# Eight-head gated attention ring: ScalarE's last masked copies, the values' high halves, VectorE's maxima and GpSimd's expert sums in another order

## The chip, the cores and the metric

The kernel runs on one core of one Trainium2 chip. The metric is device time in microseconds (us) of one execution. Six engines' rows appear in the profile: PE and PEld (TensorE's matmuls and weight loads), DVE (VectorE), ACT (ScalarE), POOL (GpSimd) and SP (SyncE). The engines run their own instruction streams in order and wait for each other through semaphores.

## The reference

Four layers run one after the other on `x` (4 batches, 256 tokens, width 128): a gated mLSTM-like attention with 4 heads, a mixture-of-experts attention with 8 heads, a cross attention with 16 heads, and a mixture of 8 feed-forward experts. The change touches the second one only:

```python
def _L0_ffn_ref(x, Wq, Wkv, Ws, Wd, Wo):       # b = 4, t = 256, H, E, DH, K = 8, 5, 64, 3
    ss = sigmoid(x @ Ws).reshape(b, t, H, E);  sd = sigmoid(x @ Wd).reshape(b, t, H, E)
    ms, md = topk_mask(ss, K), topk_mask(sd, K)
    q = einsum('bthed,bthe->bhtd', (x @ Wq)..., sd * md)
    k, v = the same of x @ Wkv with ss * ms
    attn = softmax(einsum('bhid,bhjd->bhij', q * scale, k))
    out = einsum('bhij,bhjd->bihd', attn, v)
    o5 = einsum('bthd,dm->bthm', out, Wo).reshape(b, t, H, E, DIM)
    return einsum('bthem,bthe->btm', o5, md)
```

The last two lines are computed the other way round: first z[t, e, d] = sum over heads h of md[t, h, e] * out[t, h, d], then z is multiplied by `Wo`. Products are kept near float32 by splitting operands into a high and a low float16 half.

## The kernel before, in words

**Tiling.** A batch is two tiles of 128 tokens (i = 0, 1). The 8-head layer goes through the batches in a ring of 12 steps each (`STEPS`), written as a hardware loop of three turns (`Fori(0, B - 1)`) on each engine. One turn has two halves. In the heavy half (steps 5 to 11 of batch b) the engines finish batch b's heads and project the gated queries, keys and values of batch b + 1 (the 30 chunks of `CHUNKS`). In the light half (steps 0 to 4 of batch b + 1, `HEAD_STEPS`) no chunk is projected; the experts' sum z of batch b is made and multiplied by `Wo`, beside the first heads of batch b + 1. The change is in the light half alone.

**What a step does.** In step h TensorE makes the scores of head h + 1 (L536 to L538), multiplies weights and values of head h - 3 (L560 to L562) and transposes the weights of head h - 1 (through the helper on L2056). VectorE takes the negated row maxima of head h (`nm`, L832) and the low half of the transposed weights of head h - 2 (`PTl`, L839). ScalarE copies the high half of the weights of head h - 2 (L691) and takes the exponentials of head h (L696). TensorE's scores of head h + 1 need the exponentials of head h - 1, since two PSUM banks hold the scores in turn. Its transpose of head h - 1 needs the low half of head h - 3, and the first product with the values (head 0, in step 3) needs both low halves of the values and the low half of head 0's weights.

**What else lies in the light half.**
- VectorE makes the copies of the output `ho` masked by experts 0 to 2, three instructions for a tile (`copies_z`, L870), with tile 0 ahead of step 0 and tile 1 behind step 0. Both operands lie in SBUF. Behind step 1 it takes the low halves of the values (`split_v`, two instructions, L826), again with both operands in SBUF.
- ScalarE makes the copies of experts 3 and 4 (`masked`, L711), two heads at a time. The last eight of them, and the high halves of the values (`high_v`, two instructions, L684), stand behind the exponentials of head 0.
- GpSimd sums the copies over heads for both tiles (`attend`, L964 to L967): t is the part of VectorE's copies, u that of ScalarE's. For each tile it waits for both, and then goes in turn over t and u, with a wait for its own writes behind each pair.
- TensorE transposes z of tile 0 behind step 3 and of tile 1 behind step 4, each followed by the product with `Wo` (L596). The rows of x that VectorE adds it to (L876) are what the next half waits for: TensorE takes up scores again only when both tiles are added.

**What sets the order.** Each engine's order is written by hand in `act_b`, `dve_b`, `pool_b` and `pe_b`. `POOL_STEPS_B` counts GpSimd's waits for its own writes in one turn of the loop.

Of the kernel before, what the change touches and what calls it, by code (L numbers as in the profile page):

```python
# [5 lines left out]
ALU = mybir.AluOpType  # L6
# [10 lines left out]
I = S // P  # L17
# [13 lines left out]
H1, E1, DH1, TOP = 8, 5, 64, 3  # L31
# [78 lines left out]
N_W1 = 9  # L110
N_WALL = 17
N_EARLY = 4
DVE_STEPS_B, POOL_STEPS_B, DVE_STEPS_C = 4, 16, 8


def build(nc, x, ctx_in, mask, g_x, g_f, w_i, b_i, w_f, b_f, ln_w, Wq0, Wkv0, Ws, Wd, Wo0,
          gm, bm, gl, bl, Wq1, Wk1, Wv1, Wo1, gate_w, w1, b1, w2, b2, out):
    with ExitStack() as stack:
        m, s, d = Names(), Names(), Names()
# [348 lines left out]
        T1, O1, X1 = 4 + H1, H1 // 2, len(PARTS) * I * E1  # L468
# [201 lines left out]
        def act_b(act):  # L670
# [9 lines left out]
            def high_v(b):  # L680
                act.wait_ge(s.O_ready, b * H1 + RING)
                for i in range(I):
                    act.wait_ge(s.acc_ready, b * SUMS + (4 + i + 1))
                    act.activation(m.v1h[:, i, :, 0:DH1], heads8(m.acc[:, 2, i, :]), ACT.Copy).then_inc(s.v1hi_ready, 1)  # L684
# [18 lines left out]
            def masked(b, o):  # L703

                act.wait_ge(s.O_free, b * O1 + (o + 1 + RING))
                for i in range(I):
                    for e in range(E1 - ACT_E, E1):
                        for h in (2 * o, 2 * o + 1):
                            r = slice(DH1 * h, DH1 * h + DH1)
                            at = G1 + h * E1 + e  # L710
                            ins = act.activation(m.zm[:, i, e - (E1 - ACT_E), r], m.ho[:, i, r], ACT.Copy, scale=m.topm[:, b * I + i, at:at + 1])  # L711
                    if o == O1 - 1:
                        ins.then_inc(s.z_masked, 1)
# [12 lines left out]
            with act.Fori(0, B - 1) as b:  # L726
                for h in range(HEAD_STEPS, STEPS):
                    step(b, h, True)
                    if h > HEAD_STEPS and h % 2 == 0:
                        masked(b, h // 2 - 3)  # L730
                for h in range(HEAD_STEPS):
                    step(b + 1, h, False)
                    if h == 0:
                        high_v(b + 1)
                    if h == 0:
                        masked(b, O1 - 1)
                    if h == 3:
                        copy_z(b, 0)
                    if h == 4:
                        copy_z(b, 1)  # L740
            act.wait_ge(s.z_sum, (B - 1) * I)
            act.wait_ge(s.const, 3)
            for h in range(HEAD_STEPS, STEPS):
                step(B - 1, h, False)
                for head in range(2 * (h - HEAD_STEPS), min(2 * (h - HEAD_STEPS) + 2, H1)):
                    for e in range(E1):
                        n = head * E1 + e
# [43 lines left out]
        def dve_b(dve, ch, stats, between):  # L791
# [33 lines left out]
                    dve.wait_ge(s.v1hi_ready, b * I + (i + 1))  # L825
                    dve.tensor_tensor(m.v1l[:, i, :, 0:DH1], heads8(m.acc[:, 2, i, :]), m.v1h[:, i, :, 0:DH1], ALU.subtract).then_inc(s.v1lo_ready, 1)  # L826

            def step(b, h, more):
                chunks3 = chunks_of(h) if more else ((), (), ())
                if h < H1:  # L830
                    dve.wait_ge(s.S_ready, b * H1 + (h + 1))
# [1 line left out]
                        .then_inc(s.nm_ready, 1)  # L833
                for c in chunks3[0]:
                    gate_products(b + 1, c, SUMS + b * GROUPS + c // E1)
                if 2 <= h < H1 + 2:
                    g = h - 2
                    dve.wait_ge(s.T_hi, b * T1 + (4 + g + 1))
                    dve.tensor_tensor(m.PTl[:, g % 2, :, :].rearrange("p n c -> p (n c)"), bank_T[g % 2][:, :],  # L839
                                      m.PTh[:, g % 2, :, :].rearrange("p n c -> p (n c)"), ALU.subtract).then_inc(s.T_free, 1)  # L840
# [49 lines left out]
            with dve.Fori(0, B - 1) as b:  # L890
                ch.loop(b, DVE_STEPS_B)
                for h in range(HEAD_STEPS, STEPS):
                    step(b, h, True)
                z_group = SUMS + b * GROUPS + SUMS
                copies_z(b, 0, z_group)
                for h in range(HEAD_STEPS):
                    step(b + 1, h, False)
                    if h == 0:
                        copies_z(b, 1, z_group + 1)
                    if h == 1:  # L900
                        split_v(b + 1)
                    if h == 4:
                        add_x2(b, 0)
                add_x2(b, 1)
# [25 lines left out]
        def pool_b(pool, ch, rstd, split):  # L930
# [23 lines left out]
            def attend(b):  # L954
                for k in range(SUMS):
                    sums(b + 1, k)
                for i in range(I):
                    pool.wait_ge(s.z_ready, b * I + (i + 1))
                    pool.wait_ge(s.z_masked, b * I + (i + 1))
                    E0 = E1 - ACT_E  # L960
                    t, u = (a.rearrange("p e (h c) -> p e h c", h=H1) for a in (m.prod[:, i, 0:E0, :], m.zm[:, i, :, :]))
                    z = m.z[:, i, :].rearrange("p (e c) -> p e c", e=E1)
                    for n in (4, 2):
                        pool.tensor_tensor(t[:, :, 0:n, :], t[:, :, 0:n, :], t[:, :, n:2 * n, :], ALU.add)  # L964
                        ch.link(pool.tensor_tensor(u[:, :, 0:n, :], u[:, :, 0:n, :], u[:, :, n:2 * n, :], ALU.add))
                    pool.tensor_tensor(z[:, 0:E0, :], t[:, :, 0, :], t[:, :, 1, :], ALU.add)
                    pool.tensor_tensor(z[:, E0:E1, :], u[:, :, 0, :], u[:, :, 1, :], ALU.add).then_inc(s.z_sum, 1)  # L967
                    pool.wait_ge(s.z_sum, b * I + (i + 1))
                    pool.sem_inc(s.prod_free, 1)

# [1430 lines left out]
```

## Time and profile before

| | us |
|---|---|
| median of 3 runs | 712.01 (707.45 to 712.67) |
| profiled execution | 711.09, its span 709.3 |
| PE busy in the span | 580.5 (82%) |
| DVE busy | 507.1 (71%) |
| POOL busy | 376.5 (53%) |
| ACT busy | 346.4 (49%) |
| granted TensorE clock, mean | 0.893 of full |

Times of the trace are counted from the start of the span. The three light halves start at about 198, 258 and 318 us and are over at about 219, 280 and 338 us. A row of the timeline can stand for several like instructions (xN); the times of such a row reach from the first start to the last end. What stands in brackets is how long the engine had been idle, and which instruction released it.

### The profile page before, as it was taken

The page shows a single profiled execution, that of the slowest core. Times are in us where ns is not written, and L with a number is a line of the kernel's source. Part 1 is how long each engine was busy: PE and PEld are TensorE (multiplying, and loading weights), DVE is VectorE, ACT ScalarE, POOL GpSimd, SP SyncE. Part 2 cuts the span into 40 slices and gives each one's busy share as a digit, 9 for nine tenths or more (in the row PEclk, how much of TensorE's full clock was granted, in tenths as well). Part 3 has the DMA queues.
Part 4 walks back from the last instruction along what each step waited for, and adds up shares of the span by engine and source line. Part 5 has one row for each costly group of instructions (what it writes and reads, how often), then busy time and mean ns, then how long its engine had stood idle before and what let it go on. Part 6 is the DMA issues. An engine that isn't in the chain of part 4 may idle for free. (4 is left out here: it accounts for less than half of the span.)

```text
span 709.3 us, 15705 instructions
## 1 busy us (share of the span) xinstructions
PE 580.5 (82%) x5739; PEld 391.0 (55%) x5739; DVE 507.1 (71%) x1069; ACT 346.4 (49%) x750; POOL 376.5 (53%) x340
## 2 busy tenths in 40 slices
PE   5399865769868859976747879999999999888897
PEld 5277622245344425434643446777677677666795
DVE  4936899967974982995885677776776767577653
ACT  2333300044243243425722668877877887625554
POOL 5514345663763755667447556666866665732221
PEclk9999997858968985996656999999999999999998
DMA  6311000020000000000220000000000000000000
GB/s 186 109 43 30 31 30 0 0 90 1 2 0 1 0 0 0 0 0 0 61 61 30 2 1 2 2 1 3 2 2 2 2 2 2 2 1 1 2 14 22
DMA packets 14175, 13.12 MB, mean 18 GB/s; under 512 B 3120, under 2 KB 11936, under 8 KB 14112
## 3 DMA queue, kind: packets, MB, share of 16 engines
q1 hardware_dynamic: 14112, 12.25, 5.9%
q8 instruction: 43, 0.70, 0.4%
q14 instruction: 20, 0.16, 0.1%
HBM read 11.72 MB, written 0.52 MB: 17 GB/s over the span
## 5 line engine op out<-in xcount | busy, mean ns | idle before, releaser
L1468 POOL TENSOR_TENSOR attn<-work,attn 128x512 f16<-128x512 f32 (+1 forms) x96 | 141.9, 1480 | 85.7 <-ACT attn L1275 85.7
L807 DVE TENSOR_TENSOR work<-banks,gatev 128x512 f32<-128x512 f32 x120 | 79.0, 682 | 17.0 <-PE banks L513 16.5
L1368 DVE TENSOR_REDUCE nmax<-banks 128x2 bf16<-128x1024 f32 x64 | 77.8, 1216 | 2.8 <-PE banks L1120 1.7
L511 PE MATMUL banks<-weights,xbTh 128*128 128x512 f16 x120 | 50.2, 418 | 28.4 <-DVE work L807 26.3
L1272 ACT ACTIVATE work<-banks,maskbias 128x512 f32<-128x512 f32 x64 | 44.2, 691 | 41.1 <-PE banks L1146 41.1
L2056 PE MATMUL banks<-ident,work 128*128 128x128 f32 x276 | 51.8, 325 | 8.6 <-DVE work L2256 3.0
L942 POOL TENSOR_TENSOR work<-work 128x512 f32<-128x512 f32 x24 | 30.4, 1268 | 43.9 <-DVE work L807 41.7
L1164 PE MATMUL banks<-work,attn 128*128 128x65 f16 x512 | 51.9, 196 | 1.6 <-POOL attn L1468 1.0
L1164 PEld LDWEIGHTS banks<-work,attn 128*128 128x128 f16 x512 | 48.3, 100 | 8.0 <-POOL attn L1468 4.5
L1165 PE MATMUL banks<-work,attn 128*128 128x65 f16 x512 | 52.0, 196 | 0.0
L1166 PE MATMUL banks<-work,attn 128*128 128x65 f16 x512 | 51.9, 196 | 0.0
L512 PE MATMUL banks<-weights,xbTh 128*128 128x512 f16 x120 | 49.9, 416 | 0.0
L513 PE MATMUL banks<-weights,xbTl 128*128 128x512 f16 x120 | 49.5, 412 | 0.0
L1165 PEld LDWEIGHTS banks<-work,attn 128*128 128x128 f16 x512 | 48.0, 99 | 1.8
L1166 PEld LDWEIGHTS banks<-work,attn 128*128 128x128 f16 x512 | 48.1, 99 | 0.0
L2056 PEld LDWEIGHTS banks<-ident,work 128*128 128x128 f32 x276 | 38.6, 168 | 16.8 <-issue 4.9
L511 PEld LDWEIGHTS banks<-weights,xbTh 128*128 (+1 forms) x120 | 12.1, 101 | 63.8 <-DVE work L807 56.7
L1275 ACT ACTIVATE attn<-banks,maskbias 128x512 f16<-128x512 f32 x64 | 44.2, 691 | 0.0
L946 POOL TENSOR_TENSOR work<-work 128x512 f32<-128x512 f32 x24 | 30.4, 1266 | 23.5 <-DVE work L810 23.4
L696 ACT ACTIVATE work<-banks,nm 128x256 f32<-128x256 f32 x64 | 26.5, 470 | 31.5 <-DVE nm L832 31.5
L536 PE MATMUL banks<-attn 64*128 64x256 f16 x64 | 22.2, 362 | 23.8 <-ACT work L696 14.7
L2023 POOL TENSOR_TENSOR weights<-stage,weights 128x1024 f16<-128x1024 f32 (+1 forms) x14 | 32.8, 2343 | 14.2 <-ACT weights L1917 13.6
(328 smaller groups left out, 1874.7 us busy)
## 6 DMA issues: line engine op xcount, KB each, us to landing
stage<-in_L_ffn_w SPq DMA_DIRECT2D x8, 512.0 KB, 4.0
stage<-in_L_ffn_Wkv SPq DMA_DIRECT2D x4, 640.0 KB, 4.1
stage<-in_L_ffn_Wq SPq DMA_DIRECT2D x2, 640.0 KB, 4.6
xt<-in_x SPq DMA_DIRECT2D x1, 512.0 KB, 4.4
ct<-in_ctx SPq DMA_DIRECT2D x1, 512.0 KB, 5.6
wo<-in_L_xattn_Wo SPq DMA_DIRECT2D x1, 512.0 KB
stage<-in_L_xattn_Wv SPq DMA_DIRECT2D x1, 512.0 KB, 3.6
stage<-in_L_xattn_Wq SPq DMA_DIRECT2D x1, 512.0 KB, 3.5
```

Source lines behind the costliest of these rows:

```text
L511: pe.matmul(o, xh, wh, start=True, stop=False)
L512: pe.matmul(o, xh, wl, start=False, stop=False)
L513: pe.matmul(o, xl, wh, start=False, stop=True).then_inc(s.pj_ready, 1)
L807: dve.tensor_tensor(heads8(m.prod[:, k, e, :]), heads8(bank_pj[c % 2][:, :]), wide(g, DH1), ALU.mult).then_inc(s.prod_ready, 1)
L1164: pe.matmul(o, ph, vh, start=(kt == 0), stop=False)
L1165: pe.matmul(o, ph, vl, start=False, stop=False)
L1166: ins = pe.matmul(o, pl, vh, start=False, stop=(kt == KT - 1))
L1272: act.activation(full, src, ACT.Exp, scale=DH2 ** -0.5, bias=bias)
L1275: act.activation(hi, src, ACT.Exp, scale=DH2 ** -0.5, bias=bias).then_inc(s.c_exp_done, 1)
L1368: dve.tensor_reduce(m.nmax[:, p % 2, i, :], banks[:, 6:8, :], AX.X, ALU.max, negate=True).then_inc(s.c_max_done, 1)
L1468: pool.tensor_tensor(m.Pl[:, p % 2, kts, :], m.Pf[:, kts, :], m.Ph[:, p % 2, kts, :], ALU.subtract).then_inc(s.c_P_lo, 1)
L2056: return pe.transpose(dst, src, m.ident[0:src.shape[0], 0:src.shape[0]])
```

## The change

ScalarE makes its last eight masked copies and then the high halves of the values ahead of step 0, and so ahead of the exponentials of head 0. VectorE takes the maxima of heads 0 and 1 in a row; its copies of tile 1 come behind step 1 (behind step 0 before), and the low halves of the values come inside step 2, behind the maxima of head 2 (ahead of them before). GpSimd sums u, ScalarE's experts, first, and waits for VectorE's copies only then; it waits for its own writes four times for a tile, two times before. Nothing is added or taken away but these waits.

```diff
--- before.py
+++ after.py
@@ -110,7 +110,7 @@
 N_W1 = 9
 N_WALL = 17
 N_EARLY = 4
-DVE_STEPS_B, POOL_STEPS_B, DVE_STEPS_C = 4, 16, 8
+DVE_STEPS_B, POOL_STEPS_B, DVE_STEPS_C = 4, 20, 8
 
 
 def build(nc, x, ctx_in, mask, g_x, g_f, w_i, b_i, w_f, b_f, ln_w, Wq0, Wkv0, Ws, Wd, Wo0,
@@ -728,12 +728,10 @@
                     step(b, h, True)
                     if h > HEAD_STEPS and h % 2 == 0:
                         masked(b, h // 2 - 3)
+                masked(b, O1 - 1)
+                high_v(b + 1)
                 for h in range(HEAD_STEPS):
                     step(b + 1, h, False)
-                    if h == 0:
-                        high_v(b + 1)
-                    if h == 0:
-                        masked(b, O1 - 1)
                     if h == 3:
                         copy_z(b, 0)
                     if h == 4:
@@ -825,7 +823,7 @@
                     dve.wait_ge(s.v1hi_ready, b * I + (i + 1))
                     dve.tensor_tensor(m.v1l[:, i, :, 0:DH1], heads8(m.acc[:, 2, i, :]), m.v1h[:, i, :, 0:DH1], ALU.subtract).then_inc(s.v1lo_ready, 1)
 
-            def step(b, h, more):
+            def step(b, h, more, values=False):
                 chunks3 = chunks_of(h) if more else ((), (), ())
                 if h < H1:
                     dve.wait_ge(s.S_ready, b * H1 + (h + 1))
@@ -833,6 +831,8 @@
                         .then_inc(s.nm_ready, 1)
                 for c in chunks3[0]:
                     gate_products(b + 1, c, SUMS + b * GROUPS + c // E1)
+                if values:
+                    split_v(b)
                 if 2 <= h < H1 + 2:
                     g = h - 2
                     dve.wait_ge(s.T_hi, b * T1 + (4 + g + 1))
@@ -894,11 +894,9 @@
                 z_group = SUMS + b * GROUPS + SUMS
                 copies_z(b, 0, z_group)
                 for h in range(HEAD_STEPS):
-                    step(b + 1, h, False)
-                    if h == 0:
+                    step(b + 1, h, False, values=h == 2)
+                    if h == 1:
                         copies_z(b, 1, z_group + 1)
-                    if h == 1:
-                        split_v(b + 1)
                     if h == 4:
                         add_x2(b, 0)
                 add_x2(b, 1)
@@ -955,16 +953,17 @@
                 for k in range(SUMS):
                     sums(b + 1, k)
                 for i in range(I):
-                    pool.wait_ge(s.z_ready, b * I + (i + 1))
-                    pool.wait_ge(s.z_masked, b * I + (i + 1))
                     E0 = E1 - ACT_E
                     t, u = (a.rearrange("p e (h c) -> p e h c", h=H1) for a in (m.prod[:, i, 0:E0, :], m.zm[:, i, :, :]))
                     z = m.z[:, i, :].rearrange("p (e c) -> p e c", e=E1)
+                    pool.wait_ge(s.z_masked, b * I + (i + 1))
                     for n in (4, 2):
-                        pool.tensor_tensor(t[:, :, 0:n, :], t[:, :, 0:n, :], t[:, :, n:2 * n, :], ALU.add)
                         ch.link(pool.tensor_tensor(u[:, :, 0:n, :], u[:, :, 0:n, :], u[:, :, n:2 * n, :], ALU.add))
-                    pool.tensor_tensor(z[:, 0:E0, :], t[:, :, 0, :], t[:, :, 1, :], ALU.add)
-                    pool.tensor_tensor(z[:, E0:E1, :], u[:, :, 0, :], u[:, :, 1, :], ALU.add).then_inc(s.z_sum, 1)
+                    pool.tensor_tensor(z[:, E0:E1, :], u[:, :, 0, :], u[:, :, 1, :], ALU.add)
+                    pool.wait_ge(s.z_ready, b * I + (i + 1))
+                    for n in (4, 2):
+                        ch.link(pool.tensor_tensor(t[:, :, 0:n, :], t[:, :, 0:n, :], t[:, :, n:2 * n, :], ALU.add))
+                    pool.tensor_tensor(z[:, 0:E0, :], t[:, :, 0, :], t[:, :, 1, :], ALU.add).then_inc(s.z_sum, 1)
                     pool.wait_ge(s.z_sum, b * I + (i + 1))
                     pool.sem_inc(s.prod_free, 1)
 
```

VectorE's order in a light half before, from the last copy of tile 0 to the low half of head 0's weights (`work0` is the masked copies' source, `nm` the maxima, `attn` the values' or weights' low halves):

```order
353 L870 TENSOR_TENSOR work<-work0,topm 128x512
355 L832 TENSOR_REDUCE nm<-banks 128x2 [waits s_S_ready]
358 L870 TENSOR_TENSOR work<-work0,topm 128x512
360 L870 TENSOR_TENSOR work<-work0,topm 128x512
362 L870 TENSOR_TENSOR work<-work0,topm 128x512
364 L832 TENSOR_REDUCE nm<-banks 128x2 [waits s_S_ready]
365 L826 TENSOR_TENSOR attn<-work,attn 128x8x64 [waits s_v1hi_ready]
367 L826 TENSOR_TENSOR attn<-work,attn 128x8x64 [waits s_v1hi_ready]
369 L832 TENSOR_REDUCE nm<-banks 128x2 [waits s_S_ready]
371 L839 TENSOR_TENSOR attn<-banks,attn 128x512 [waits s_T_hi]
```

And the same place now:

```order
353 L870 TENSOR_TENSOR work<-work0,topm 128x512
355 L830 TENSOR_REDUCE nm<-banks 128x2 [waits s_S_ready]
357 L830 TENSOR_REDUCE nm<-banks 128x2 [waits s_S_ready]
360 L870 TENSOR_TENSOR work<-work0,topm 128x512
362 L870 TENSOR_TENSOR work<-work0,topm 128x512
364 L870 TENSOR_TENSOR work<-work0,topm 128x512
366 L830 TENSOR_REDUCE nm<-banks 128x2 [waits s_S_ready]
367 L824 TENSOR_TENSOR attn<-work,attn 128x8x64 [waits s_v1hi_ready]
369 L824 TENSOR_TENSOR attn<-work,attn 128x8x64 [waits s_v1hi_ready]
371 L839 TENSOR_TENSOR attn<-banks,attn 128x512 [waits s_T_hi]
```

The second maxima have moved ahead of the three copies of tile 1, and the third ahead of the two low halves; the instructions are the same ten.

GpSimd's order for tile 0 before (`s_z_masked` is ScalarE's signal, `s_z_ready` VectorE's, `s_pool_chain` its own):

```order
140 L964 TENSOR_TENSOR work<-work 128x3x256 [waits s_acc_ready,s_z_masked,s_z_ready]
141 L965 TENSOR_TENSOR work<-work 128x2x256
143 L964 TENSOR_TENSOR work<-work 128x3x128 [waits s_pool_chain]
144 L965 TENSOR_TENSOR work<-work 128x2x128
146 L966 TENSOR_TENSOR z<-work 128x192 [waits s_pool_chain]
147 L967 TENSOR_TENSOR z<-work 128x128
```

And now:

```order
140 L961 TENSOR_TENSOR work<-work 128x2x256 [waits s_acc_ready,s_z_masked]
142 L961 TENSOR_TENSOR work<-work 128x2x128 [waits s_pool_chain]
144 L962 TENSOR_TENSOR z<-work 128x128 [waits s_pool_chain]
145 L965 TENSOR_TENSOR work<-work 128x3x256 [waits s_z_ready]
147 L965 TENSOR_TENSOR work<-work 128x3x128 [waits s_pool_chain]
149 L966 TENSOR_TENSOR z<-work 128x192 [waits s_pool_chain]
```

The three sums of u stand ahead of the three of t, and the wait for VectorE's copies stands between them.

## Rows read from the trace of the kernel before

**Rows 1.** TensorE, timeline, first light half: start, us, engine, line, operation, idle before.

```profile
202.16 0.37 PE L536 MATMUL banks<-attn 64*128 64x256 f16 x1 [2.54 <-ACT work L696]
...
205.82 0.37 PE L536 MATMUL banks<-attn 64*128 64x256 f16 x1 [1.18 <-ACT work L696]
...
209.62 0.24 PE L560 MATMUL banks<-attn 128*128 128x65 f16 x1
...
211.94 0.39 PE L536 MATMUL banks<-attn 64*128 64x256 f16 x1
...
216.64 0.55 PE L2056 MATMUL banks<-ident,z 128*128 128x128 f32 x3 [1.77 <-POOL z L967]
...
219.69 0.37 PE L536 MATMUL banks<-attn 64*128 64x256 f16 x1 [0.75 <-DVE xt L876]
```

**Rows 2.** Line 967 (GpSimd's last sum): who waited for it (us, times).

```profile
  PE banks L2056: 3.5, 2
```

**Rows 3.** GpSimd, timeline, first light half.

```profile
197.53 1.26 POOL L946 TENSOR_TENSOR work<-work 128x512 f32<-128x512 f32 x1 [0.77 <-DVE work L810]
204.15 2.26 POOL L964 TENSOR_TENSOR work<-work 128x768 f32<-128x768 f32 x1 [5.36 <-ACT work L711]
...
210.73 1.80 POOL L964 TENSOR_TENSOR work<-work 128x768 f32<-128x768 f32 x1 [0.24 <-POOL z L967]
212.49 1.27 POOL L965 TENSOR_TENSOR work<-work 128x512 f32<-128x512 f32 x1
213.83 0.99 POOL L964 TENSOR_TENSOR work<-work 128x384 f32<-128x384 f32 x1
214.78 0.72 POOL L965 TENSOR_TENSOR work<-work 128x256 f32<-128x256 f32 x1
215.58 0.59 POOL L966 TENSOR_TENSOR z<-work 128x192 f32<-128x192 f32 x1
216.13 0.45 POOL L967 TENSOR_TENSOR z<-work 128x128 f32<-128x128 f32 x1
```

**Rows 4.** ScalarE, timeline, first light half.

```profile
201.18 0.84 ACT L696 ACTIVATE work<-banks,nm 128x256 f32<-128x256 f32 x2 [4.31 <-DVE nm L832]
...
202.94 2.01 ACT L711 ACTIVATE work<-work,topm 128x64 f32<-128x64 f32 x8
```

**Rows 5.** VectorE, timeline, first light half.

```profile
197.97 2.57 DVE L870 TENSOR_TENSOR work<-work,topm 128x512 f32<-128x512 f32 x3
200.47 0.68 DVE L832 TENSOR_REDUCE nm<-banks 128x2 f32<-128x512 f32 x1
201.07 1.88 DVE L870 TENSOR_TENSOR work<-work,topm 128x512 f32<-128x512 f32 x3
...
203.47 1.27 DVE L826 TENSOR_TENSOR attn<-work,attn 128x512 f16<-128x512 f32 x2
...
206.19 0.69 DVE L839 TENSOR_TENSOR attn<-banks,attn 128x512 f16<-128x512 f32 x1 [0.84 <-ACT attn L691]
```

**Rows 6.** GpSimd's weight splits beside VectorE's low halves, before the loop, timeline.

```profile
146.70 1.49 POOL L2021 TENSOR_SCALAR wq1h<-stage 128x1024 f16<-128x1024 f32 x1
148.28 2.43 POOL L2023 TENSOR_TENSOR wq1l<-stage,wq1h 128x1024 f16<-128x1024 f32 x1
```

**Rows 7.** VectorE in the same stretch, timeline.

```profile
145.12 3.61 DVE L826 TENSOR_TENSOR attn<-work,attn 128x512 f16<-128x512 f32 x2
```

**Rows 8.** TensorE, timeline, second light half.

```profile
271.70 0.39 PE L536 MATMUL banks<-attn 64*128 64x256 f16 x1
...
280.62 0.37 PE L536 MATMUL banks<-attn 64*128 64x256 f16 x1 [0.75 <-DVE xt L876]
```

**Rows 9.** Busy us by stretch, granted clock (PEclk), DMA share, GB/s.

```profile
212.00:219.00 7.00, 4.54 (x38) 3.23 (x37) 1.04 (x2) 2.85 (x8) 4.42 (x6) 0.96 0.01 2
219.00:226.00 7.00, 6.31 (x32) 3.50 (x33) 3.76 (x9) 1.36 (x3) 1.20 (x1) 0.53 0.00 0
274.00:281.00 7.00, 5.62 (x21) 4.05 (x21) 1.15 (x3) 1.10 (x3) 2.27 (x4) 0.50 0.00 0
```

## Prediction

> **What bounds the kernel now.** I read the page's parts 1 and 2 first: no engine is full, so the question is what ends the stretch that the change touches. Then the timelines of the first light half, engine by engine, and the second light half for comparison.
>
> TensorE is in the chain at both ends. It waits 2.54 us for the exponentials of head 0, 1.18 for those of head 1, and near the end 1.77 for GpSimd's last sum; only 0.75 us behind x's last addition do scores go on, at 219.69 [rows 1]. The wait for GpSimd decides in two of the three turns, 3.5 us in all [rows 2]; in the other TensorE comes to that place later than GpSimd is done. GpSimd had been idle 5.36 us before its first sum of z, until ScalarE's masked copies came, and then works from 204.15 to 216.58 [rows 3]. ScalarE made those copies late: it idled 4.31 us, so from 196.87, until the maxima of head 0, and placed the eight copies at 202.94, behind exponentials and high halves [rows 4]. VectorE is in the light half's front, not in its end: copies, maxima, copies, low halves in a line [rows 5].
>
> **ScalarE's part.** The eight copies (2.01 us) now go from 196.87 to 198.9. The high halves follow when GpSimd's last projection sum is done, 197.53 + 1.26 = 198.79 [rows 3], and take under 1.3: the 1.76 us from 201.18 to 202.94 held them and most of the exponentials' 0.84. They are over by 200.2. The exponentials of head 0 cannot start before 201.15, the end of the maxima (200.47 + 0.68) [rows 4, 5]. So this move costs nothing; if the cover went it would cost at most the 3.2 us of both pieces.
>
> **GpSimd's part.** u of tile 0 can start at 198.79 and a little. One tile takes 1.80 + 1.27 + 0.99 + 0.72 + 0.59 + 0.45 = 5.82 us, and 0.24 between tiles [rows 3]. The four links in place of two put gaps of 0.08 (213.83 + 0.99 to 214.78 overlaps by 0.04; 214.78 + 0.72 to 215.58 leaves 0.08) where there were overlaps of 0.04: 0.12 x 2 = 0.24 us more for a tile. Undisturbed, GpSimd would be done near 199.1 + 2 x 5.9 + 0.24 = 211.1 to 211.8, some 5 us earlier than now. The wait of 1.77 goes in either case.
>
> **The price: the two engines hinder each other.** VectorE's three copies of tile 0 took 2.57 us, those of tile 1 1.88 [rows 5]. The difference is the first of them: copies follow each other at 0.60, so it ended at 197.97 + 2.57 - 1.20 = 199.34, which is 0.55 behind the end of GpSimd's sum at 198.79. The other way round, GpSimd's first sum took 2.26 where its twin took 1.80 [rows 3]: it began in effect at 204.61, 0.13 ahead of the end of VectorE's low halves (203.47 + 1.27 = 204.74) [rows 5]. Before the loop the two alternate: two low halves took 3.61 instead of 1.27, and GpSimd's operation between them 1.49 (to 148.19, VectorE 0.54 later) [rows 6, 7]. So a VectorE instruction with both operands in SBUF and a GpSimd sum exclude each other and take turns. Maxima and the low halves of the weights, which read PSUM, show nothing of the kind: 0.68 and 0.69 at 200.47 and 206.19, the latter beside GpSimd's sums [rows 3, 5].
>
> Before, GpSimd was silent while VectorE made its copies, because ScalarE was late. Now u and t run beside eight such instructions. By the two offsets, in the first turn (us of the trace before):
> - copy 1 ends 199.34 as before. u's first sum has waited since about 199.1: 199.21 to 200.48. Copy 2 ends 201.03, u's second sum 201.62, copy 3 202.17, u's last 202.50.
> - Maxima of head 0: 202.07 to 202.75 (before 201.15, so 1.6 late). Maxima of head 1 to 203.35. t's first sum 202.45 to 204.25.
> - Tile 1's copies end 204.80, 206.21, 207.22, between t's sums that end 205.66 and 206.67. Maxima of head 2 end 207.80.
> - u of tile 1 from 207.09 to 208.36; low half of the values 208.91; u 209.50; low half 210.05; u's last 210.38. Low half of head 0's weights 209.95 to 210.63, where it was 206.19 to 206.88: 3.76 us late. Maxima of head 3 end 211.23.
>
> **TensorE behind it.** Scores came 1.01 us behind the end of the maxima of head 0 (202.16 - 201.15) and, without the wait of 1.18, 2.48 behind each other (205.82 - 1.18 - 202.16) [rows 1]. So scores of head 2 at 203.76, of head 3 at 206.24 (the exponentials of head 1 are long done, which is what the two maxima in a row bring: the loss of 1.6 shrinks to 0.42), of head 4 at 207.80 + 1.01 = 208.81. Its first product with the values needs the low half at 210.63: with the 0.12 to 0.14 of such a release, 210.75, before 209.62. From there to the scores of head 5 it was 211.94 - 209.62 = 2.32: 213.07, so **1.13 us later** than before. Without any exclusion it would be 1.18 earlier.
>
> From there to the next half's scores: 219.69 - 211.94 - 1.77 = 5.98 us at a granted clock of mostly 0.96, and 280.62 - 271.70 = 8.92 in the second turn, at 0.50, the lower of the two levels [rows 1, 8, 9]. With each turn's clock as it was, turns 1 and 3 gain 1.77 - 1.13 = 0.64 each, turn 2 loses 1.13: together -0.15 us.
>
> **What the clock may add.** After this end the first turn ran at 0.53 from 219 to 226, PE busy 6.31 of 7 [rows 9]. The full clock would take at most half of it, 3.1, and VectorE (3.76 of 7 busy) leaves room. TensorE is idle less just ahead of it now (the 1.77 is gone), so I take 1 us for each of the first two turns, between 0 and 3.1: -2 us. Ahead of its busy stretch TensorE idles 1.6 longer than before, but from 203.76 on it is nearly without a gap. The Trainium skill's page "TensorE: Matmul & The Clock Gate" (Part 1, "What's actually happening") has the throttled state as the default and activity as what releases it; by that rule the denser stretch would tend to bring the full clock earlier, where the second turn's rows show a dense stretch at 0.50 all the same.
>
> The sum: -0.15 - 2 = -2.2 us against the profiled execution's 711.09 (its span 709.3 and 1.8 around it), so 708.9; that execution lies 0.9 below the median of 712.01, on which scale it is 709.8, rounded to **710.0**.
>
> The skill's page "SBUF — State Buffer" ("A bandwidth-pool intuition that's wrong") has the loser of the shared port start about 115 ns behind VectorE's end; the row here shows 0.13 ahead of it. By the page's figure each of the eight waiting sums would come 0.245 later, an estimate of 2.0 us a turn on VectorE's line and some 6 in all, which would give 716. I go by the row.
>
> **The rivals.**
> - *No price for the overlap* (chance 0.17). If VectorE's instructions mostly slip between the sums, all three turns gain the 1.18, and turns 1 and 3 the 1.77 too: 2 x 2.95 + 1.18 = 7.1 us, so 704.9, and 703 with the clock's 2. For it: a race at 199.1 to 199.2 for the second copy is close. Against it: rows 6 and 7 show the alternation.
> - *The lower clock to the end* (chance 0.20). TensorE is granted 1.2 GHz from the scores of head 5 on in all three turns, as it was in the second [rows 8, 9]. Then the end takes 8.92 instead of 5.98: turns 1 and 3 lose 1.13 + 2.94 - 1.77 = 2.30, turn 2 loses 1.13: 5.7 us slower, 717.7. It decides from the point where the lower clock holds for over 0.64 / 2.94 = 22% of that end. With a later half also slow it passes 719.
> - *GpSimd's wait was no bound* (chance 0.08): what VectorE loses is all there is, 3 x 1.13 = 3.4 slower, 715.4. Against it: the 1.77 stands directly in TensorE's row.
>
> The forecast's own case has the rest, 0.55. Its own range is 706 to 714: each turn between -2.2 and +1.1 with the clock, and the runs of before alone span 5.2 us. Over all cases the range is **703.5 to 717.5**. A change of 1% (7.1 us) is about what a measurement of this kernel tells from none. Faster by more: half of the first rival and a tail of the forecast's case with the full clock kept twice, 0.15. Slower by more: a third of the second rival, little else, 0.09. Within 1%: 0.76.
>
> **What the changed profile would show.** Right: GpSimd's first sum of z at about 199.2 and its last over before 215; VectorE's copies of tile 0 at over 4 us for three, its low halves of the values at over 2 us for two; the maxima of head 0 near 202; no wait of TensorE for GpSimd in front of tile 1's transpose; TensorE's wait for exponentials of head 1 gone, and a wait for VectorE in front of the first product with the values. Wrong: maxima of head 0 still near 200.5 and head 5's scores near 210.8 (the first rival), or the clock at 0.5 up to x's addition in all three turns (the second). What would upset it most is a step of the clock that falls elsewhere in the heavy halves, which no row here can fix.

## The result: 0.3% slower

| | median us (runs) | ratio to before, 95% interval |
|---|---|---|
| before | 713.04 (707.45 to 715.19, 20 runs) | |
| changed | 715.14 (713.75 to 717.66, 20 runs) | 1.0033 (1.0019 to 1.0048) |

The changed kernel is slower by 2.1 us. The forecast was 2 us faster; the time lies within its range, the direction is wrong. All ratios leave out runs that lie over 1.5% above the fastest of the same kernel, which concerns three of six runs in experiment 1 and in experiment 7 and none elsewhere. The profiled execution took 714.6 us, its span is 712.9 with a mean granted clock of 0.879 (before: 711.09, 709.3, 0.893).

The timeline of VectorE in the changed kernel's first light half (start us, us, engine, line, operation, idle before):

```profile
199.94 4.18 DVE L870 TENSOR_TENSOR work<-work,topm 128x512 f32<-128x512 f32 x3
204.04 1.28 DVE L830 TENSOR_REDUCE nm<-banks 128x2 f32<-128x512 f32 x2
205.24 3.92 DVE L870 TENSOR_TENSOR work<-work,topm 128x512 f32<-128x512 f32 x3
209.08 0.68 DVE L830 TENSOR_REDUCE nm<-banks 128x2 f32<-128x512 f32 x1
209.68 2.29 DVE L824 TENSOR_TENSOR attn<-work,attn 128x512 f16<-128x512 f32 x2
211.89 0.68 DVE L839 TENSOR_TENSOR attn<-banks,attn 128x512 f16<-128x512 f32 x1
```

The same of GpSimd, whose first sum of z stood at 204.15 before [rows 3]:

```profile
200.94 2.63 POOL L961 TENSOR_TENSOR work<-work 128x512 f32<-128x512 f32 x2 [0.18 <-POOL work L944]
203.65 0.78 POOL L962 TENSOR_TENSOR z<-work 128x128 f32<-128x128 f32 x1
204.39 3.20 POOL L965 TENSOR_TENSOR work<-work 128x768 f32<-128x768 f32 x2
...
215.19 0.59 POOL L966 TENSOR_TENSOR z<-work 128x192 f32<-128x192 f32 x1
```

And of TensorE, for [rows 1]:

```profile
205.74 0.37 PE L536 MATMUL banks<-attn 64*128 64x256 f16 x1 [4.37 <-ACT work L696]
...
208.15 0.39 PE L536 MATMUL banks<-attn 64*128 64x256 f16 x1
...
215.11 0.39 PE L536 MATMUL banks<-attn 64*128 64x256 f16 x1
...
218.20 0.55 PE L2055 MATMUL banks<-ident,z 128*128 128x128 f32 x3
219.37 1.13 PE L596 MATMUL banks<-wo,zT 128*128 128x128 f32 x6 [0.63 <-ACT zT L719]
221.25 0.27 PE L536 MATMUL banks<-attn 64*128 64x256 f16 x1 [0.75 <-DVE xt L876]
```

This light half begins 1.97 us later than in the trace before, because of a heavy half in which nothing is changed (below), so 1.97 is taken off every time for the comparison. Then the maxima of head 0 start at 202.07 (forecast 202.07), tile 1's copies end at 207.19 (207.22), the maxima of head 2 end at 207.79 (207.80), the low half of head 0's weights ends at 210.60 (210.63), scores of head 5 start at 213.14 (213.07) and the next half's scores at 219.28 (219.05). The three copies of a tile take 4.18 and 3.92 us where they took 2.57 and 1.88 [rows 5], the two low halves of the values 2.29 where they took 1.27. TensorE no longer waits for the exponentials of head 1, nor for GpSimd.

All three turns, in two profiled executions of each kernel. "Light" reaches from VectorE's first copy to the end of the second addition to x, "heavy" from there to the next first copy, "tail" from the end of light 3 to the end of the layer's last addition:

| us | light 1 | heavy | light 2 | heavy | light 3 | tail | sum |
|---|---|---|---|---|---|---|---|
| before | 21.47 | 38.30 | 22.64 | 36.96 | 21.47 | 40.08 | 180.9 |
| before, second profile | 22.65 | 36.99 | 21.47 | 38.36 | 22.67 | 39.70 | 181.8 |
| changed | 21.06 | 35.32 | 23.77 | 37.21 | 23.77 | 40.91 | 182.0 |
| changed, second profile | 22.31 | 36.85 | 23.78 | 37.22 | 23.78 | 40.91 | 184.9 |

The same instructions in the same order take one of a few lengths, and the length goes with the granted clock. The next rows give busy time by stretch (length of the stretch, busy us of PE, PEld, DVE, ACT, POOL, then the granted clock PEclk, DMA share, GB/s). They are of the changed kernel: the second half of its light half 1, the start of the heavy half behind it, and the end of light half 2.

```profile
208.00:219.00 11.00, 10.04 (x68) 6.66 (x66) 7.40 (x11) 4.83 (x12) 7.29 (x7) 0.63 0.01 1
219.00:226.00 7.00, 5.88 (x45) 3.66 (x46) 3.94 (x9) 2.32 (x6) 1.26 (x1) 1.00 0.00 0
...
268.00:280.00 12.00, 10.38 (x59) 7.43 (x57) 4.02 (x8) 3.68 (x10) 3.99 (x4) 0.50 0.00 0
```

The clock rose within light half 1 and stayed up (1.00 from 219 to 226, where it was 0.53 before [rows 9]): light 21.06, heavy 35.32. In light halves 2 and 3 it stayed at the lower level, 1.2 GHz, to their end: 23.77 twice, exactly the 2.30 us more than 21.47 that the second rival gave for such a turn.

The 1.97 us come from the heavy half ahead of light half 1, where nothing is changed. The clock was up by 165 us in the trace before and rose later than that in the changed one. First before, then changed:

```profile
165.00:170.00 5.00, 5.00 (x50) 3.22 (x49) 4.77 (x11) 2.71 (x9) 2.54 (x2) 1.00 0.00 0
```

```profile
165.00:170.00 5.00, 5.00 (x32) 2.94 (x31) 3.48 (x8) 1.91 (x6) 1.26 (x1) 0.66 0.00 0
```

Two profiles of one kernel differ by some 1 to 3 us in the three turns alone (180.9 and 181.8, 182.0 and 184.9), and the 20 runs are what shows the 2.1.

### The profile page after: what moved, and what is told of

Read it like the earlier page. It is cut to its first block and busy times, and to the rows that moved or that the text cites. A ratio compares the mean times of both kernels' runs of the same rounds, so it can differ in the third digit from the quotient of the medians.

```text
span 712.9 us, 15711 instructions
## 1 busy us (share of the span) xinstructions
PE 584.9 (82%) x5739; PEld 394.9 (55%) x5739; DVE 522.8 (73%) x1069; ACT 347.8 (49%) x750; POOL 383.4 (54%) x340
## 5 line engine op out<-in xcount | busy, mean ns | idle before, releaser
L677 ACT ACTIVATE attn<-banks 128x512 f16<-128x512 f32 x16 | 9.1, 596 | 64.5 <-PE banks L2055 64.5
```

## The experiments

The first four experiments set two theories against each other. **A**: a GpSimd sum and a VectorE instruction with both operands in SBUF exclude each other, and the change loses by that. **B**: the exclusion costs nothing in the end, the clock alone differs. Ratios are to the kernel before, run in the same session. The edits of these four are shown against the changed kernel; `...` stands for lines left out.

### 1. GpSimd's part undone

```diff
+                    pool.wait_ge(s.z_ready, b * I + (i + 1))
+                    pool.wait_ge(s.z_masked, b * I + (i + 1))
...
-                    pool.wait_ge(s.z_masked, b * I + (i + 1))
                     for n in (4, 2):
+                        pool.tensor_tensor(t[:, :, 0:n, :], t[:, :, 0:n, :], t[:, :, n:2 * n, :], ALU.add)
                         ch.link(pool.tensor_tensor(u[:, :, 0:n, :], u[:, :, 0:n, :], u[:, :, n:2 * n, :], ALU.add))
...
-                    pool.wait_ge(s.z_ready, b * I + (i + 1))
```

> The changed kernel with GpSimd's part undone: it waits for VectorE's copies of a tile before any sum, and sums t and u in turn, as before. ScalarE's and VectorE's parts stay. Theory A (a GpSimd sum and a VectorE instruction with both operands in SBUF exclude each other; the changed kernel loses because u runs beside the copies of tile 0): copies 2 and 3 of tile 0 are free of GpSimd again, the three take 2.6 us, maxima of head 0 end at their place before (3.2 us behind the first copy's start), low half of head 0's weights ends about 1.8 us earlier than in the changed kernel, scores of head 5 some 0.5 us earlier than in the kernel before; total 708 to 710 us. Theory B (the changed kernel is slower by the lower TensorE clock alone, the exclusion costs nothing in the end): within 0.3% of the changed kernel, 713.5 to 717.

Measured: 708.99 us (700.43 to 712.4, six runs). The runs fall into two groups, 700.43 to 706.78 at a mean clock of 0.896 to 0.901, and 711.21 to 712.40 at 0.882 to 0.887. The ratio to before, 0.9873 (0.9828 to 0.9919), is that of the first group; by the medians of all runs it is 708.99 / 711.98 = 0.996. It is faster than the changed kernel in either count. That it is faster than the kernel before rests on the first group: the mean of all six is 3.9 us below that of before, with a standard error of 2.1. VectorE and GpSimd in its second light half:

```profile
257.67 2.58 DVE L870 TENSOR_TENSOR work<-work,topm 128x512 f32<-128x512 f32 x3
260.17 1.27 DVE L830 TENSOR_REDUCE nm<-banks 128x2 f32<-128x512 f32 x2
261.37 4.38 DVE L870 TENSOR_TENSOR work<-work,topm 128x512 f32<-128x512 f32 x3
...
267.88 0.68 DVE L839 TENSOR_TENSOR attn<-banks,attn 128x512 f16<-128x512 f32 x1
```

```profile
260.33 1.80 POOL L962 TENSOR_TENSOR work<-work 128x768 f32<-128x768 f32 x1 [1.83 <-DVE work L870]
```

GpSimd now starts behind tile 0's copies, these take 2.58 again, and the low half of head 0's weights ends 10.89 us behind the first copy, between before (8.91) and the change (12.61 to 12.63). Its three light halves take 22.06, 19.58 and 19.58 us at mean clocks of 0.54, 0.65 and 0.65. Theory A's number (708 to 710) holds, B's (713.5 to 717) does not.

### 2. VectorE's part undone

```diff
-                    step(b + 1, h, False, values=h == 2)
-                    if h == 1:
+                    step(b + 1, h, False)
+                    if h == 0:
                         copies_z(b, 1, z_group + 1)
+                    if h == 1:
+                        split_v(b + 1)
```

> The changed kernel with VectorE's part undone: copies of tile 1 between the maxima of heads 0 and 1, low halves of the values ahead of the maxima of head 2. Theory A: the maxima of head 1 now stand behind three copies that each wait for a GpSimd sum, so they end some 4.4 us later than in the changed kernel, and scores of head 5 come 2.2 us later in each turn: 720 to 723 us. Theory B: the order of maxima and copies moves VectorE work by 1.8 us at most, 714 to 717 us.

Measured: 714.95 us (713.57 to 717.56), 1.0064 (1.0035 to 1.0093). A miss of theory A in the total, by 5 us: it is no slower than the changed kernel. The wait that theory A forecast is there, though. TensorE waits for the exponentials of head 0 and of head 1 in its first light half:

```profile
204.91 0.37 PE L536 MATMUL banks<-attn 64*128 64x256 f16 x1 [4.37 <-ACT work L696]
...
209.95 0.37 PE L536 MATMUL banks<-attn 64*128 64x256 f16 x1 [2.55 <-ACT work L696]
```

That light half had the lower clock to its end and took 25.95 us, 2.18 more than the changed kernel's 23.77 at the same level, as expected (2.2). The other two had the full clock at their end and took 23.10 and 22.91, again about 2 more than the changed kernel's at that level (21.06), but less than the 23.77 that it took in two turns of three. I had worked out the work and left the clock as it was; the clock did not stay.

### 3. ScalarE's part undone

```diff
-                masked(b, O1 - 1)
-                high_v(b + 1)
                 for h in range(HEAD_STEPS):
                     step(b + 1, h, False)
+                    if h == 0:
+                        high_v(b + 1)
+                    if h == 0:
+                        masked(b, O1 - 1)
```

> The changed kernel with ScalarE's part undone: the last masked copies and the values' high halves behind the exponentials of head 0. Theory A: GpSimd can begin only some 6 us behind VectorE's first copy, so all six copies are free of it (2.6 and 1.9 us for three) and only the low halves of the values meet it; GpSimd is again what TensorE waits for at tile 1's transpose; as the kernel before or 0.3 us a turn slower: 713 to 715 us. Theory B: same total as the changed kernel or better, 711 to 716, with no change in the copies' times.

Measured: 717.32 us (716.72 to 718.19), 1.0093 (1.0066 to 1.0121), the slowest of all, and above the range of either theory (713 to 715, 711 to 716). The copies are free of GpSimd (2.58 and 1.88 us) and the low halves meet it (2.79), as theory A has it. The light halves take 23.20, 23.21 and 23.20 us, each at a mean clock of 0.56 and with a wait for GpSimd at the end (0.54 us in the first), and the heavy halves 38.30 and 38.29. So what the three parts are worth does not add up part by part: GpSimd's late start binds again, and no turn of this profile had the higher clock at its end.

### 4. Most of GpSimd's sums of z left out

This kernel leaves out eight of the twelve sums of a turn, so its z is that of heads 0 and 1 alone.

```diff
-                    for n in (4, 2):
-                        ch.link(pool.tensor_tensor(u[:, :, 0:n, :], u[:, :, 0:n, :], u[:, :, n:2 * n, :], ALU.add))
...
-                    for n in (4, 2):
-                        ch.link(pool.tensor_tensor(t[:, :, 0:n, :], t[:, :, 0:n, :], t[:, :, n:2 * n, :], ALU.add))
```

> The changed kernel with eight of GpSimd's twelve sums of z in a turn left out (the additions of 4 and of 2 head groups; z is then the sum of heads 0 and 1 only). It shows what the changed order would give if GpSimd hardly used SBUF. Theory A: copies of a tile take 2 to 3 us, maxima of head 0 are late by at most 0.5 us, scores of head 5 come 0.9 us earlier than in the kernel before and 2 us earlier than in the changed one, and the end is not GpSimd's: 705 to 709 us. Theory B: GpSimd's work has no part in VectorE's times; 713 to 717 us.

Measured: 709.78 us (707.52 to 711.08), 0.9978 (0.9956 to 1.0000). VectorE's copies of its second light half:

```profile
257.43 2.84 DVE L870 TENSOR_TENSOR work<-work,topm 128x512 f32<-128x512 f32 x3
...
261.39 1.94 DVE L870 TENSOR_TENSOR work<-work,topm 128x512 f32<-128x512 f32 x3
```

4.18 and 3.92 became 2.84 and 1.94 by taking work from GpSimd alone: the exclusion is shown. The low half of head 0's weights ends 8.42 to 9.27 us behind the first copy. So the total is 5 us below the changed kernel's. Yet the light halves were 21.63, 20.78 and 21.64 us, at mean clocks of 0.55, 0.59 and 0.54, and the total is 0.8 us above the expected range. The experiment that removes nearly the whole price of the overlap is no faster than experiment 1, which keeps a good part of it but had 0.65 in two light halves. That the clock makes up the difference is read from these two profiles; experiments 10 to 12 test it.

### 5 to 7. Idle matmuls in the gaps at the start

An idle matmul is one whose result nobody reads; here 16 and 20 (32 on the changed kernel) of them fill TensorE's first two waits of a light half. **C**: the clock hangs on TensorE's gaps at the start of a light half. **D**: it does not, or does not matter.

```diff
+            def warm(n):
+                for _ in range(n):
+                    pe.matmul(bank_O[1][:, 264:512], m.xbTh[:, 0, :], m.wkv0h[:, 0:248], start=True, stop=True)
...
+                pe.wait_ge(s.O_free, b * O1 + O1 + RING)
+                warm(16)
                 scores(b + 1, 0)
                 for h in range(HEAD_STEPS):
                     step(b + 1, h, False)
+                    if h == 0:
+                        warm(20)
```

On the kernel before:

> The kernel before, with idle matmuls (their results are read by nobody) in TensorE's two gaps at the start of each light half: 16 ahead of the first scores and 20 ahead of the scores of head 2. Theory C (the granted clock of the light half and of the start of the heavy half behind it hangs on these gaps): granted clock near 1.0 in all three light halves; each takes 21.5 us from VectorE's first copy to the second addition (GpSimd's sums bound it), each heavy half 35.3 us; some 6 us less in all, 706 to 708. Theory D (the clock is set by something else, or no longer matters once GpSimd is the bound): 711 to 714, with 20 idle matmuls possibly delaying the scores of head 2 by up to 1.5 us a turn.

On the changed kernel:

> The changed kernel with the same idle matmuls, 16 and 32, since its second gap is 4.4 us. Theory C: clock near 1.0 in all light halves; VectorE's line (low half of head 0's weights 12.6 us behind its first copy) is unchanged and bounds; light halves of 20 to 20.5 us, heavy halves of 35.3; 704 to 707 us, so that with the clock held the changed order is faster than the order before. Theory D: 714 to 717 us.

On experiment 1's:

> GpSimd's part undone, ScalarE's and VectorE's kept, and the idle matmuls (16 and 20). Theory C: light halves of 19 to 19.5 us, heavy halves of 35.3, 701 to 704 us, the fastest of all. Theory D: as without the idle matmuls, 707 to 711.

Measured: 713.45 us, 1.0017 (0.9993 to 1.0040); 714.77 us, 1.0040 (1.0012 to 1.0068); 709.04 us, 0.9862 (0.9821 to 0.9903). Each is about the time of the same kernel without fillers (713.04, 715.14, 708.99). Theory C falls as I had put it, and the stretches of the changed kernel with fillers show why:

```profile
200.00:204.00 4.00, 3.63 (x38) 3.07 (x37) 4.00 (x4) 2.03 (x7) 3.66 (x4) 1.00 0.01 2
204.00:208.00 4.00, 3.06 (x26) 2.13 (x24) 4.00 (x5) 2.06 (x5) 3.84 (x4) 1.00 0.00 0
208.00:212.00 4.00, 1.55 (x12) 0.92 (x10) 4.00 (x5) 1.43 (x4) 3.67 (x4) 1.00 0.00 0
212.00:216.00 4.00, 2.79 (x22) 2.29 (x23) 2.62 (x5) 1.21 (x4) 3.84 (x4) 0.63 0.01 4
```

```profile
211.04 0.27 PE L536 MATMUL banks<-attn 64*128 64x256 f16 x1 [2.31 <-ACT work L704]
```

The clock did hold to 212, while without fillers the scores at 205.74 already took 0.37 instead of 0.27. TensorE then did its scores faster and waited for the exponentials that VectorE's line sets: a new gap of 2.31 us ahead of the scores of head 4, PE busy 1.55 of 4, and a clock of 0.63 for what came behind it. The two other kernels show the same, with new gaps of 2.26 and 2.77 us. The light halves are 21.14, 23.85 and 23.80, against 21.06, 23.77 and 23.77. While VectorE's line binds, a faster TensorE gains nothing; behind it TensorE itself binds, and there the clock was low again.

### 8 and 9. Both kernels once more

> The changed kernel once more, for a second profile. Both theories: VectorE's times in each light half as in the first (maxima of head 0 start 4.1 us and low half of head 0's weights ends 12.6 us behind the first copy). Theory C: where the granted clock rises differs from the first profile in at least one of the three turns, and that turn's light half takes 21.1 us with the rise ahead of its end and 23.8 without; nothing between the first copy and the end takes other values than by this clock.

> The kernel before once more, for a second profile. VectorE's and GpSimd's times in each light half as in the first (maxima of head 0 start 2.5 us, the low half of head 0's weights ends 8.9 us behind the first copy). Each light half is 21.5 us, or 22.7 where the lower clock holds to its end, and the pattern over the three turns may differ from the first profile.

Measured: 715.86 and 713.21 us, one run each; they are the rows called second profile in the table above. The changed kernel's maxima of head 0 start 4.10 us and the low half of head 0's weights ends 12.61 us behind the first copy in every turn, of before 2.50 and 8.92. One expectation was too strict: light half 1 of the changed kernel took 22.31, neither 21.1 nor 23.8. The clock rose late in it (0.54 from 214 to 218, 0.89 from 218 to 222). Of its three light halves, the kernel before had the lower clock to the end in one in the first profile and in two in the second, the changed kernel in two in both.

### 10 to 12. Idle matmuls in all gaps up to the scores of head 5

**E**: what counts is the clock behind the last gap. **F**: it falls all the same. Fillers as above, and more ahead of the scores of head 4 (18 on the changed kernel, 20 on experiment 1's) or of head 3 (18 on the kernel before), and ahead of the first product with the values (11, 3 and 5 on the same three). In all it is 77, 59 and 59 in a light half. The edit on the changed kernel, beyond that of experiment 6:

```diff
+                warm(fill)
                 if 3 <= h < H1 + 3:
...
-                    step(b + 1, h, False)
+                    step(b + 1, h, False, 11 if h == 3 else 0)
...
+                    if h == 2:
+                        warm(18)
```

On experiment 1's:

> GpSimd's part undone and idle matmuls in all of TensorE's gaps of a light half up to the scores of head 5: 16 and 20 as in the run before, 20 more ahead of the scores of head 4 and 3 ahead of the first product with the values. Theory E (what counts is the granted clock behind the last gap, where TensorE has no more waiting to hide it in; the first fillers only moved the fall of the clock to the middle): clock near 1.0 to the end of each light half, light halves of 19 to 19.6 us, heavy halves of 35.3, 700 to 704 us. Theory F (the clock falls all the same, or the fillers get in the way): 707 to 711, as without them.

On the changed kernel:

> The changed kernel with idle matmuls in all gaps: 16, 32, 18 ahead of the scores of head 4, 11 ahead of the first product with the values. Theory E: light halves of 20 to 21 us in all three turns and heavy halves of 35.3, 704 to 708 us. Theory F: 714 to 717.

On the kernel before:

> The kernel before with idle matmuls in all gaps: 16, 20, 18 ahead of the scores of head 3, 5 ahead of the first product with the values. Theory E: the light halves end by GpSimd at 21.5 us in all three turns, heavy halves 35.3: 706 to 709 us, so 1 to 3 us behind the changed kernel with its gaps filled, since with the clock held the changed order is the shorter one. Theory F: 712 to 715, and ahead of the changed kernel as without fillers.

| | median us | ratio to before | light halves | heavy halves |
|---|---|---|---|---|
| experiment 1's, filled | 706.88 (705.14 to 709.95) | 0.9933 (0.9904 to 0.9962) | 19.59, 19.57, 19.58 | 38.35, 38.39 |
| changed, filled | **701.69** (699.77 to 708.99) | 0.9869 (0.9823 to 0.9916) | 19.62, 19.60, 19.62 | 35.30, 35.28 |
| before, filled | 713.04 (712.33 to 715.73) | 1.0022 (0.9997 to 1.0047) | 22.29, 22.66, 22.29 | 37.12, 37.86 |

The changed kernel, filled, in its first turn, stretches and TensorE's timeline:

```profile
208.00:219.00 11.00, 9.17 (x89) 6.91 (x87) 7.00 (x11) 5.01 (x13) 6.14 (x6) 1.00 0.00 0
219.00:226.00 7.00, 6.99 (x60) 3.93 (x58) 5.75 (x13) 4.05 (x13) 2.54 (x2) 1.00 0.00 0
```

```profile
209.41 0.27 PE L536 MATMUL banks<-attn 64*128 64x256 f16 x1 [0.39 <-ACT work L709]
...
212.83 0.27 PE L536 MATMUL banks<-attn 64*128 64x256 f16 x1
...
218.43 0.27 PE L536 MATMUL banks<-attn 64*128 64x256 f16 x1 [0.75 <-DVE xt L889]
```

For the changed order theory E holds, and the time is even below its range (704 to 708). With the clock up to the end all its light halves are 19.6 us, though VectorE's line is as long as ever (12.64), and the heavy halves 35.3. The changed kernel so filled is the fastest of all by its median, 12 to 13 us faster than without fillers (by the ratios to before, and by the medians of two sessions). For the two others theory E's numbers fail: 706.88 is above 700 to 704, and 713.04 above 706 to 709, within theory F's 712 to 715. With TensorE at full speed they wait for GpSimd, which starts later there, and no filler stands in that wait. The kernel before, and then experiment 1's, both filled:

```profile
218.90 0.55 PE L2069 MATMUL banks<-ident,z 128*128 128x128 f32 x3 [2.99 <-POOL z L980]
220.08 1.95 PE L601 MATMUL banks<-wo,zT 128*128 128x128 f32 x6 [0.63 <-ACT zT L732]
```

```profile
216.86 0.55 PE L2067 MATMUL banks<-ident,z 128*128 128x128 f32 x3 [1.65 <-POOL z L978]
218.03 1.13 PE L601 MATMUL banks<-wo,zT 128*128 128x128 f32 x6 [0.63 <-ACT zT L732]
219.90 0.37 PE L536 MATMUL banks<-attn 64*128 64x256 f16 x1 [0.75 <-DVE xt L889]
```

In the kernel before, behind 2.99 us of waiting, the last product takes 1.95 us instead of 1.13; in experiment 1's, behind 1.65 us, that product still takes 1.13, but the next half's scores take 0.37 instead of 0.27. The heavy halves behind are 2 to 3 us longer than 35.3. The changed kernel's GpSimd sums u early and is not waited for, and its heavy halves start with the full clock. So with the gaps up to the scores of head 5 filled it is 701.69 against 713.04: the changed order is 11 us better with these fillers, and 2 us worse without.

Not all of the 11 is the order's. The fillers are not the same in number, and the kernel before had no filler in its wait of 2.99, so its clock did not hold to the end. If it did, an estimate from the rows is 22.29 - (1.95 - 1.13) = 21.47 for a light half and 35.3 for a heavy one, and the changed order would lead by 3 x (21.47 - 19.6), some 6 us. No run tests this.

## Why the prediction was wrong

- *What bounds the kernel.* Right: the 1.77 and the 1.18 us are gone, GpSimd is no bound any more.
- *ScalarE's part costs nothing.* Right: its high halves are over at 201.79 in the trace (199.8 on the scale of before), 2.97 us ahead of the exponentials. Of the three parts it is the one whose undoing costs most (experiment 3): without it GpSimd starts late.
- *The exclusion.* Right in kind and size: eight steps of the walk come out within 0.1 us, and taking GpSimd's sums away takes the time away (experiment 4). The first rival (no price) is refuted. The offset from the row served. The Trainium skill's page "SBUF — State Buffer" ("A bandwidth-pool intuition that's wrong") has the blocked side held until about 115 ns behind VectorE's end, measured there on a DMA whose descriptors GpSimd writes; by that figure the low half of head 0's weights would have come an estimated 2.0 us later than it did, so the trace of these sums does not agree.
- *1.13 us later at the scores of head 5.* Right: 1.2 in turn 1, 23.77 - 22.64 = 1.13 for the whole light half where both had the lower clock.
- ***"With each turn's clock as it was": this step failed.*** It gave -0.15 us for the three light halves. Their sum was 65.6 and 66.8 us in the two profiles before and 68.6 and 69.9 in those of the change: +3.05 by the means. What the order is worth depends on the clock: -0.41 (21.06 for 21.47) with the higher clock at the end, +1.13 with the lower, and +2.30 where the lower one took the place of the higher. The changed kernel had the lower one to the end in four of its six profiled light halves, and in part in a fifth; the kernel before in three of six.
- ***The tail, a term put at nothing without a reason, failed too.*** It took 40.91 us twice, for 40.08 and 39.70: +1.02. Some 0.8 of it is one product with `Wo` of the last batch, which got the lower clock in both profiles of the changed kernel and the full one in both of the kernel before. Before, then changed:

```profile
373.65 1.13 PE L596 MATMUL banks<-wo,zT 128*128 128x128 f32 x6 [0.79 <-ACT zT L719]
```

```profile
375.94 1.95 PE L596 MATMUL banks<-wo,zT 128*128 128x128 f32 x6 [0.79 <-ACT zT L719]
```

- *"What the clock may add", -2.* The two heavy halves between the turns took 75.3 us in both profiles before and 72.5 and 74.1 in those of the change: -2.0 by the means. The size is the forecast's, but there is luck in it. A clear gain came once, 35.32 for 38.30; the other three took 36.85, 37.21 and 37.22, where the four before took 36.96 to 38.36. Behind a light half that ended at the lower clock there was none (37.21 and 37.22, for 36.96 and 36.99).
- The three differences add up to +3.05 + 1.02 - 2.00 = +2.07 us, where the 20 runs have +2.1. With two profiles each this near agreement is luck as well: the whole times of the same four executions differ by 3.1, so 1.0 of it lies outside the turns.
- *The rivals.* The second (lower clock to the end in all turns, 717.7) describes what happened in two turns of three; I gave it 0.20, though the one slow turn in three of the only trace argued for more. The third came nearest by number, 715.4, but by luck: it has GpSimd's wait as no bound, and with the full clock at the end of both, the light half without that wait is 0.41 us shorter although VectorE is late.

What stays open: why the full clock comes in one turn and not in another of the same program, and so whether the change itself makes the lower clock more frequent; four of six against three of six does not show it. The rows show that the clock was lower behind waits of 1.65, 2.31 and 2.99 us that stood behind filled gaps, and that in the changed kernel, with all these gaps filled, it was up to the end of all three light halves.

## What to carry to other kernels

Where an engine is let start earlier, look at what the other engines do in that time: here a VectorE instruction with both operands in SBUF and a GpSimd sum took turns, each paying for the other (4.18 us for 2.57). Starting GpSimd behind the first of the VectorE work on which the chain hangs gave back 1.7 of the 3.7 us that VectorE's line had lost, and a total 6 us shorter (experiment 1). And where TensorE waits for others, price the turn at both clock levels: filling the gaps at the start only moved the gap (experiments 5 to 7), and the gain came when the stretch that TensorE itself binds, behind the last gap, was reached with the clock up (experiment 11).

## What the runs showed that I had not expected

- 77 idle matmuls in a light half (16, 32, 18, 11) take the changed kernel from 715.14 to 701.69 us; the first 48 alone leave it at 714.77.
- A faster TensorE made its own gaps: at the full clock up to 212 us, it waited 2.31 us for exponentials where it had waited about 0.1 at half the clock.
- Filled, the changed kernel and experiment 1's have light halves of equal length, 19.6, though VectorE's line is 1.7 us longer in the first (12.64 for 10.90). What tells them apart is a wait of 1.65 us for GpSimd at the end of the second, and with it the clock at the start of the heavy half behind: 38.4 us for 35.3. The order that is better without fillers is 5 us slower with them.
